# A graph-attention and mixture-of-experts layer: register loads without tests, accumulators read a step later, expert weights prepared earlier, another opening, and column groups of 8, 8, 8, 5 and 3 tiles

## The chip, the cores and the metric

One NeuronCore of one Trainium2 chip runs the whole kernel. The metric is device time in microseconds (us); less is better. Five engines work side by side, each on its own list in program order: TensorE (PE), VectorE (DVE), ScalarE (ACT), GpSimd (POOL) and SyncE (SP), which only issues transfers. They meet through semaphores alone.

## The reference

```python
def reference(x, adj, ...):            # x 4096 x 128, adj 4096 x 4096, int32, about 1% ones
    h  = layernorm(x)
    Wh = h @ W_w + W_b
    e  = leaky_relu((Wh @ a1)[:, None] + (Wh @ a2)[None, :], 0.2)
    x  = x + softmax(where(adj > 0, e, -9e15), axis=1) @ Wh
    h  = layernorm(x)
    top2, idx = top_k(h @ Wg.T + bg, 2)     # 8 experts, hidden width 512
    c  = softmax(top2) placed at idx
    return x + sum_e c[:, e] * (relu(h @ W1[e].T + b1[e]) @ W2[e].T + b2[e])
```

## The kernel before

**Attention.** The 4096 output rows are 32 column tiles of 128, taken in five supergroups of 8, 8, 8, 6 and 2 tiles (`WB`). Each supergroup goes through all 32 source tiles: 160 steps, numbered n. A step is one instruction on DVE, `weigh` (L779), which makes the unnormalised weights `prob` of one source tile against all columns of the supergroup, and on PE `attend` (L1283), one matmul per column tile into accumulators that stay in PSUM for the whole supergroup; fp32, so the profile has two passes for each. `prob` has 6 buffers, and DVE's list runs 4 steps ahead of PE's. The mask comes from the int32 adjacency: SP loads a chunk (2 steps of an 8- or 6-wide supergroup, 8 steps of the 2-wide one), and ACT turns it into bf16 (`edges`, L1111, its list 6 steps ahead). There are 4 chunk buffers and 4 mask buffers.

**The opening.** x is normalised, transposed (L1244, groups of four tiles), projected (L1251), and multiplied once more for the row term of the scores (L1255). ACT takes exponentials (`keep_s`), DVE stores `Wh` (`keep_Wh`). Groups 0 and 1 go through this ahead of step 0, groups 2 to 7 inside the steps of supergroup 0. A run-time flag, `narrow`, chooses between a short and a general way of making the weights; each engine loads it into a register and branches.

**End of a supergroup.** DVE adds the accumulators out of PSUM (`evacuate`, L849), and over the next 14 steps `finish` (parts p = 0 to 13, one a step) makes the rows x1, normalises them (xn, L885, at p = 4 and 5), has PE transpose them (L1397, p = 5 and 6), scores the experts (p = 7 and 8), ranks them, and writes slots, `offs` and `etab` (p = 11 to 13). PE cannot start the next supergroup before the accumulators are read, nor pass p = 5 before xn is there. Then POOL sends the rows to `xbuf` in DRAM, sorted by expert, with two indirect transfers for each column tile (`send`, L627, from 12 steps on; 8 steps on for the last supergroup, two to a step).

**Experts.** 71 tiles of 128 sorted rows (`NT`) follow, in five rounds; a round's tiles are those which are sure to be full after its supergroup, numbers 0, 9, 25, 41 and 53 being the first of each. SP loads a tile's rows (`load_slab`, L445 and L446) at a row number that it reads from `offs` into a register, five beats ahead of its use, six buffers; PE transposes (`turn`, L1323), multiplies up (L1351 to L1353) and down (L1370 to L1382); ACT and DVE split the hidden values into high and low fp16 parts (L1158, L996) and scale the result; POOL computes the target rows and scatters them to `ybuf` (`give_back`, L640). PE's work on a tile is cut into 14 pieces which lie between the matmuls of two steps. Tiles up to 35 are done that way. From step 160 on (`TAIL`, tile 36) a beat is one tile and nothing else, the last 35 tiles; and there SP also copies each tile's first-layer weights into the free mask buffers (`copy_weights`, L457 and L458), eight tiles ahead, at an address read from `etab`. PE reads the same table (`fetch`, L1331). The last supergroup's `finish` lies in steps 160 to 169.

**Other work put into the lists by step number.** Expert weights are loaded, shifted on POOL (L559), and split on ACT and DVE (L1121, L836) from step 20 + 6e on for expert e (`expert_at`). `add_bias` (L552, POOL) is at the steps of `bias_at`. In step 141 SP fills the ends of the expert regions with zeros (`fill_ends`, L431 and L432, eight transfers). At the end SP reads `ybuf` back, DVE adds, and the result is stored.

A register load with bounds is written `value_load(..., min_val=, max_val=)`.

Of the kernel before, what the change touches and what calls it, by code (L numbers as in the profile page):

```python
# [5 lines left out]
def build(nc, x, adjT, W, Wb, a, WgT, bg, wcat, wlast, b2, out):  # L6
# [7 lines left out]
    E = WgT.shape[1]  # L14
# [8 lines left out]
    WB = [8, 8, 8, 6, 2]  # L23
# [3 lines left out]
    STEPS = SG * TILES  # L27
    FW = F + 1
# [42 lines left out]
    chunks = [(g, u, min(8, 2 * SB // WB[g])) for g in range(SG) for u in range(0, TILES, min(8, 2 * SB // WB[g]))]  # L71
# [38 lines left out]
    with ctx:  # L110
# [194 lines left out]
        s_wlo = sem("s_wlo")  # L305
        s_G = sem("s_G")
# [87 lines left out]
        def _(sp):  # L394
# [11 lines left out]
            def load_chunk(m, general):  # L406
                if m >= AR:
                    if general:
                        sp.wait_ge(s_P, chunk_end[m - AR])
                    else:  # L410
                        sp.wait_ge(s_G, m - AR + 1)
# [23 lines left out]
            def load_slab(t):  # L435
# [9 lines left out]
                row = sp.value_load(offs[0:1, t:t + 1], min_val=0, max_val=ROWS - P)  # L445
                sp.dma_start(slab[t % XR][:, :], xbuf[bass.ds(row, P), :]).then_inc(s_ld[t % XR], 16)  # L446

            def copy_weights(t, general):
# [8 lines left out]
                e = sp.value_load(etab[0:1, t:t + 1], min_val=0, max_val=(E - 1) * EW)  # L457
# [42 lines left out]
            with sp.If(fast != 0):  # L500
                load_chunk(2, False)
                load_chunk(3, False)
                main(False)
            with sp.Else():
                for i in range(2):
                    sp.wait_ge(s_adj[i], 16)
                sp.wait_ge(s_G, 1)
# [181 lines left out]
        def _(dve):  # L689
# [34 lines left out]
            def keep_Wh(i):  # L724
# [19 lines left out]
            nc.vector.tensor_tensor(wsq[:, :], wa[:, 1:2], wa[:, 1:2], ALU.mult).then_inc(s_was, 1)  # L744
            nc.vector.tensor_copy(Wx[:, F:FW], wa[:, 1:2])
# [4 lines left out]
            normalise(1)  # L750
# [18 lines left out]
            def weigh(n):  # L769
# [6 lines left out]
                dve.wait_ge(s_G, m + 1)  # L776
# [5 lines left out]
            def row_maxima(g):  # L782

                if g == 0:
                    dve.wait_ge(s_whs, GROUPS)
                    dve.wait_ge(s_G, 1)
# [28 lines left out]
            def weigh_general(n):  # L815
# [13 lines left out]
                dve.wait_ge(s_adj[m % AR], 16 * (m // AR + 1 + (m % AR < 2)))  # L829
# [169 lines left out]
            def main(general):  # L999
                for n in range(-LB, NS):  # L1000
                    m = n + LB
                    ends = 0 <= n < STEPS and n % TILES == TILES - 1
                    if ends and not general:
                        evacuate(n // TILES)
                    if m < STEPS and (m or general):
                        (weigh_general if general else weigh)(m)
                    if ends and general:
                        evacuate(n // TILES)
                    if not general:
# [3 lines left out]
                        i = group_at(n, 3)  # L1013
# [478 lines left out]
```

## Time and profile before

| | us |
|---|---|
| median of 3 runs (lowest, highest) | 511.89 (507.74, 513.55) |
| the profiled execution, its own time | 510.71 |
| its span | 508.9 |
| PE busy, 4079 matmuls | 420.4 |
| DVE busy, 874 instructions | 361.3 |
| ACT busy | 259.6 |
| POOL busy | 238.3 |
| chain that ended last: PE 53%, SP's queue 13%, "issue" 12%, DVE 9%, DMA 6% | |

Supergroups 0 to 4 end on PE at about 101.2, 171.4, 261.5, 346.0 and 400.2 us. The last tile's result is ready at 484, and what follows is reading back, adding and storing. A busy share says little here, because each stretch has another limit: read the stretches one by one. SP has no busy time in the profile; its queue is seen only in the timeline and in the chain.

### The profile page before, as it was taken

The page shows a single profiled execution, that of the slowest core. Times are in us where ns is not written, and L with a number is a line of the kernel's source. Part 1 is how long each engine was busy: PE and PEld are TensorE (multiplying, and loading weights), DVE is VectorE, ACT ScalarE, POOL GpSimd, SP SyncE. Part 2 cuts the span into 40 slices and gives each one's busy share as a digit, 9 for nine tenths or more (in the row PEclk, how much of TensorE's full clock was granted, in tenths as well). Part 3 has the DMA queues.
Part 4 walks back from the last instruction along what each step waited for, and adds up shares of the span by engine and source line. Part 5 has one row for each costly group of instructions (what it writes and reads, how often), then busy time and mean ns, then how long its engine had stood idle before and what let it go on. Part 6 is the DMA issues. An engine that isn't in the chain of part 4 may idle for free.

```text
span 508.9 us, 12723 instructions
## 1 busy us (share of the span) xinstructions
PE 420.4 (83%) x4079; PEld 389.7 (77%) x4079; DVE 361.3 (71%) x874; ACT 259.6 (51%) x382; POOL 238.3 (47%) x298
## 2 busy tenths in 40 slices
PE   2679999977999759999997999998897986777800
PEld 1479999977999749999997999997886875555700
DVE  5297868999999998976659696547692668344526
ACT  2398678625746507554544745534643464455600
POOL 3412310513288420478824258873466648545510
PEclk9999999997999989999999999999898989999965
DMA  7889687983999835846462566513175545444258
GB/s 230 335 281 311 229 295 259 373 300 128 354 332 369 330 144 183 268 143 227 154 211 91 161 210 205 197 50 95 54 214 145 192 140 176 159 150 145 73 168 334
DMA packets 39164, 107.01 MB, mean 210 GB/s; under 512 B 6557, under 2 KB 17825, under 8 KB 32437
## 3 DMA queue, kind: packets, MB, share of 16 engines
q1 hardware_dynamic: 32468, 91.36, 53.0%
q0 software_dynamic: 4320, 8.47, 4.8%
q10 hardware_dynamic: 2304, 6.29, 3.6%
q8 instruction: 38, 0.62, 0.5%
q14 instruction: 34, 0.27, 0.2%
HBM read 84.57 MB, written 13.07 MB: 192 GB/s over the span
## 4 chain that ended last, share of the span: by engine, by line
PE 53%; SPq 13%; issue 12%; DVE 9%; DMA 6%; ACT 3%; POOL 3%; POOLq 0%; DVEq 0%; ACTq 0%
PE acc L1283 38%; DVE prob L779 3%; SPq L458 3%; DMA slab<-xbuf 2%; SPq L445 2%; SPq L457 2%; DMA adj<-ybuf 2%; PE yt L1251 2%; SPq L446 2%; PE m L1255 2%; POOL ybuf L640 2%; DMA adj<-adjT 1%; PE hps L1351 1%; PE hps L1353 1%; PE hps L1352 1%
## 5 line engine op out<-in xcount | busy, mean ns | idle before, releaser
L1283 PE MATMUL acc<-Wh,prob 128*128 128x129 f32 x2048 | 298.8, 288 | 4.7 <-DVE num L849 4.7
L1283 PEld LDWEIGHTS acc<-Wh,prob 128*128 128x128 f32 x2048 | 264.2, 195 | 9.6 <-issue 4.8
L779 DVE SCALAR_TENSOR_TENSOR prob<-s_bc,E_col,G_all 128x1024 f32<-128x1024 f32 (+2 forms) x160 | 178.8, 1136 | 24.0 <-PE acc L1283 22.8
L1111 ACT ACTIVATE G_all<-adj 128x2048 bf16<-128x2048 int32 (+1 forms) x68 | 122.1, 1803 | 22.7 <-DVE prob L779 16.2
L640 POOL DMA_INDIRECT ybuf<-wst,dest x71 | 74.1, 1043 | 72.7 <-ACT wst L1165 34.0
L627 POOL DMA_INDIRECT xbuf<-xr,slot x64 | 81.3, 1270 | 49.0 <-PE acc L1283 34.2
L996 DVE SCALAR_TENSOR_TENSOR wst<-hps,wst 128x512 f16<-128x512 f32 x71 | 49.0, 690 | 65.2 <-ACT wst L1158 63.8
L1158 ACT ACTIVATE wst<-hps 128x512 f16<-128x512 f32 x71 | 42.2, 594 | 18.5 <-PE hps L1353 14.7
L1153 ACT ACTIVATE xT<-yt 128x256 f16<-128x256 f16 x71 | 27.2, 382 | 32.4 <-PE yt L1323 31.8
L1165 ACT ACTIVATE wst<-yt,slab 128x128 f32<-128x128 f32 x36 | 13.2, 367 | 56.8 <-PE yt L1382 56.7
L559 POOL TENSOR_TENSOR wst<-wst,wlb 127x512 f32<-127x512 f32 x8 | 13.5, 1681 | 43.1 <-DMA wlb<-wlast 43.0
L1351 PE MATMUL hps<-xT,wall 128*128 128x128 f16 x148 | 32.6, 224 | 1.1 <-ACT xT L1153 0.6
L1353 PE MATMUL hps<-xT,wall 128*128 128x128 f16 x148 | 32.7, 224 | 0.0
L1352 PE MATMUL hps<-xT,wall 128*128 128x128 f16 x148 | 32.5, 223 | 0.0
L1323 PE MATMUL yt<-ident,slab 128*128 128x128 f16 x142 | 19.8, 221 | 15.0 <-DMA slab<-xbuf 14.0
L538 POOL TENSOR_TENSOR scratch<-scratch,mhalf 128x4 f32<-128x4 f32 x8 | 12.0, 1506 | 40.6 <-DVE scratch L713 40.6
L610 POOL TENSOR_TENSOR rstd<-ve,mhalf 128x4 f32<-128x4 f32 (+2 forms) x10 | 12.1, 1208 | 36.8 <-DVE ve L878 36.6
L1372 PE MATMUL yt<-wall,wst 128*128 x144 | 28.9, 225 | 0.0
L1370 PE MATMUL yt<-wall,wst 128*128 x144 | 28.7, 225 | 0.0
L1375 PE MATMUL acc<-wall,wst 128*128 x140 | 23.6, 283 | 4.7 <-issue 3.3
L1382 PE MATMUL yt<-wall,wst 128*128 x144 | 26.7, 220 | 0.0
L1323 PEld LDWEIGHTS yt<-ident,slab 128*128 128x128 f16 x142 | 11.8, 99 | 18.7 <-DMA slab<-xbuf 16.7
(177 smaller groups left out, 616.7 us busy)
## 6 DMA issues: line engine op xcount, KB each, us to landing
adj<-adjT SPq DMA_DIRECT2D x52, 1024.0 KB
adj<-adjT SPq DMA_DIRECT2D x16, 768.0 KB
G_all<-wall SPq DMA_DIRECT2D x34, 256.0 KB, 2.4
slab<-xbuf SPq DMA_DIRECT2D x71, 65.0 KB, 2.4
wst<-wcat ACTq DMA_DIRECT2D x8, 512.0 KB, 5.4
adj<-ybuf SPq DMA_DIRECT2D x8, 512.0 KB, 7.6
xs<-x SPq DMA_DIRECT2D x8, 256.0 KB, 9.4
wlb<-wlast ACTq DMA_DIRECT2D x8, 256.0 KB, 6.5
```

Of the source, the lines that this page charges most:

```text
L627: nc.gpsimd.indirect_dma_start(xbuf[:, :], bass.IndirectOffsetOnAxis(ap=slot[:, w, b:b + 1].bitcast(u32), axis=0), xr[:, w, b, :], None).t ...
L640: nc.gpsimd.indirect_dma_start(ybuf[:, :], bass.IndirectOffsetOnAxis(ap=dest[:, t:t + 1].bitcast(u32), axis=0), ysb[t % YR][:, :], None, b ...
L779: nc.vector.scalar_tensor_tensor(prob[n % PR][:, 0:w], c_bc[:, P * AT[g]:P * AT[g] + w], E_col[:, u:u + 1], G[m % GR][:, k * w:(k + 1) * w ...
L996: nc.vector.scalar_tensor_tensor(h_lo[t % 2][:, :], hps[t % 2][:, :], 0.0, h_hi[t % 2][:, :], op0=ALU.max, op1=ALU.subtract).then_inc(s_hl, 1)
L1111: nc.scalar.activation(G[m % GR][:, 0:w], adj_sb[m % AR][:, 0:w], ACT.Relu).then_inc(s_G, 1)
L1158: nc.scalar.activation(h_hi[t % 2][:, :], hps[t % 2][:, :], ACT.Relu).then_inc(s_hh, 1)
L1283: last = nc.tensor.matmul(acc_of(b), prob[n % PR][:, b * P:(b + 1) * P], Wh[:, u, :], start=(u == 0 and b % 3 == 0), stop=(u == TILES - 1) ...
L1323: last = nc.tensor.transpose(tps[:, h * P:(h + 1) * P], x16[:, h * P:(h + 1) * P], ident16[:, :])
L1351: nc.tensor.matmul(dst, whi, xhi, start=(k == 0), stop=False, skip_group_check=True)
L1352: nc.tensor.matmul(dst, whi, xlo, start=False, stop=False, skip_group_check=True)
L1353: last = nc.tensor.matmul(dst, wlo, xhi, start=False, stop=True, skip_group_check=True)
L1372: nc.tensor.matmul(yps, hi[:, ks], weights(t, 2 * HID + 2 * j * P + P), start=False, stop=False, skip_group_check=True)
```

## The change

Register loads of `offs` and `etab` carry their bounds as a statement and no longer as a test at run time (those of `fill_ends` stay). `evacuate` stands one step later in DVE's list, so the weights of one more step come ahead of it. Everything at `expert_at` comes 12 steps earlier, and `add_bias` 2 to 14 steps earlier. The last two supergroups are 5 and 3 tiles wide; the 3-wide one has chunks of 4 steps. The rounds then begin at tiles 0, 9, 25, 41 and 51. In the opening DVE makes the first mask, chunks 2 and 3 are asked for without a wait, the score row comes ahead of the projection, and the projection of group 1 and the work of groups 2 to 7 lie a step later in PE's list. The zero fill of `xbuf`'s spare rows moves from step 4 to step 64. (Column spans on the host follow; no arithmetic there.)

```diff
-    WB = [8, 8, 8, 6, 2]
+    WB = [8, 8, 8, 5, 3]
+    WIDE = [2, 2, 2, 2, 4]
-    chunks = [(g, u, min(8, 2 * SB // WB[g])) for g in range(SG) for u in range(0, TILES, min(8, 2 * SB // WB[g]))]
+    chunks = [(g, u, WIDE[g]) for g in range(SG) for u in range(0, TILES, WIDE[g])]
...
         def expert_at(n, part):
-            e, r = divmod(n - part - 20, 6)
+            e, r = divmod(n - part - 8, 6)
...
-        bias_at = {n: i for i, n in enumerate([28, 30, 58, 60, 90, 92, 122, 124])}
+        bias_at = {n: i for i, n in enumerate([26, 28, 44, 46, 84, 86, 116, 118])}
...  SP
-                row = sp.value_load(offs[0:1, t:t + 1], min_val=0, max_val=ROWS - P)
+                row = sp.value_load(offs[0:1, t:t + 1]).with_bounds(min_val=0, max_val=ROWS - P)
...
-                e = sp.value_load(etab[0:1, t:t + 1], min_val=0, max_val=(E - 1) * EW)
+                e = sp.value_load(etab[0:1, t:t + 1]).with_bounds(min_val=0, max_val=(E - 1) * EW)
...
-            for g in range(4, GROUPS):
+            load_chunk(2, False)
+            load_x(4)
+            load_chunk(3, False)
+            for g in range(5, GROUPS):
                 load_x(g)
...
-                    if n == 4:
+                    if n == 2 * TILES:
                         sp.wait_ge(s_const, 13)
                         sp.dma_start(xbuf[E * CAP:ROWS, :]...          # zero fill of spare rows
...  DVE
+            normalise(1)
             nc.vector.tensor_copy(Wx[:, F:FW], wa[:, 1:2])
...
-            normalise(1)
             dve.wait_ge(s_reach, 1)
...
+            dve.wait_ge(s_adj[0], 16)
+            nc.vector.tensor_scalar(G[0][:, :], adj_sb[0][:, :], 0.0, None, ALU.max).then_inc(s_G0, 1)
             stats(2)
-            stats(3)
...
-                    ends = 0 <= n < STEPS and n % TILES == TILES - 1
+                    ends = 0 < n <= STEPS and n % TILES == 0
                     if ends and not general:
-                        evacuate(n // TILES)
+                        evacuate(n // TILES - 1)
                     if m < STEPS and (m or general):
                         (weigh_general if general else weigh)(m)
...
-                        i = group_at(n, 3)
+                        i = 1 if n == -1 else group_at(n, 3)
                         if i is not None:
                             keep_Wh(i)
...
-                keep_Wh(0)
                 group_row(0)
                 weigh(0)
-                keep_Wh(1)
+                keep_Wh(0)
+                stats(3)
                 main(False)
...  ACT
-            def keep_s(i, general):
+            def keep_E(i):                 # the two exponentials of the projection
                 act.wait_ge(s_wh, i + 1)
...
+            def keep_s(i, general):        # the score row
                 act.wait_ge(s_sm, i + 1)
+                row = acc[2] if i == 1 else m1
...
-                        i = group_at(n, 1)
+                        i = group_at(n, 2)
                         if i is not None:
                             keep_hT(i)
-                        i = group_at(n, 2)
+                        if n == -1:
+                            keep_E(1)
+                        i = group_at(n, 3)
                         if i is not None:
+                            keep_E(i)
                             keep_s(i, general)
...
-            edges(0)
             keep_hT(0)
             keep_hT(1)
...  PE
+            transposes(0)
             pe.wait_ge(s_was, 2)
             nc.tensor.matmul(m1[:, P + 3:P + 4], ones[:, :], wsq[:, :], start=True, stop=True).then_inc(s_tq, 1)
-            transposes(0)
+            transposes(1)
             pe.wait_ge(s_was, 3)
             pe.wait_ge(s_tqs, 1)
+            project_s(0)
+            project_s(1)
             project(0)
-            transposes(1)
-            project(1)
...
-                place[t] = pe.value_load(etab[0:1, t:t + 1], min_val=0, max_val=(E - 1) * EW)
+                place[t] = pe.value_load(etab[0:1, t:t + 1]).with_bounds(min_val=0, max_val=(E - 1) * EW)
...
-                        i = group_at(n, 0)
+                        i = group_at(n, 1)
                         if i is not None:
                             transposes(i)
-                        i = group_at(n, 2)
+                        if n == 1:
+                            project(1)
+                        i = group_at(n, 3)
                         if i is not None:
                             project(i)
+                            project_s(i)
```

## Rows read from the trace of the kernel before

**Rows 1.** Stages: length, busy us per engine (instructions), granted PE clock, DMA share, GB/s.
```profile
29.23:101.20 71.97, 71.97 (x595) 68.92 (x594) 59.10 (x89) 56.15 (x73) 18.40 (x20) 1.00 0.86 295
101.20:171.40 70.20, 62.56 (x546) 62.01 (x545) 68.07 (x141) 37.20 (x25) 35.14 (x26) 0.95 0.84 308
261.50:346.00 84.50, 80.85 (x856) 77.80 (x854) 59.44 (x153) 42.22 (x66) 49.38 (x54) 1.00 0.50 157
346.00:400.20 54.20, 46.27 (x486) 41.63 (x484) 36.10 (x132) 24.14 (x45) 30.99 (x39) 0.94 0.46 135
400.20:485.80 85.60, 65.87 (x799) 51.90 (x796) 45.61 (x130) 45.23 (x107) 48.87 (x77) 0.98 0.43 143
```
**Rows 2.** Chain of waits, start and length in us: one register test on SP.
```profile
426.11 0.15 SPq L445
...
426.38 0.04 SPq L446
```
**Rows 3.** Instructions of line 499, the load of the flag, written without bounds.
```profile
L499 SPq TENSOR_LOAD <-narrow x1: 471/471/471, 12.4 to 12.4; - x1
```
**Rows 4.** Two stretches of the last 35 tiles, columns as in rows 1.
```profile
440.00:470.00 30.00, 22.13 (x268) 16.67 (x267) 12.08 (x24) 15.37 (x36) 14.49 (x24) 1.00 0.46 151
474.00:480.00 6.00, 5.93 (x82) 4.92 (x81) 3.43 (x7) 4.09 (x11) 2.77 (x5) 1.00 0.27 68
```
**Rows 5.** SP's timeline (start, length): row loads of tiles 40, 41, 51 and 67.
```profile
395.83 0.35 SPq L446 DMA_DIRECT2D slab<-xbuf  x1
...
404.14 0.33 SPq L446 DMA_DIRECT2D slab<-xbuf  x1
...
430.29 0.35 SPq L446 DMA_DIRECT2D slab<-xbuf  x1
...
472.21 0.35 SPq L446 DMA_DIRECT2D slab<-xbuf  x1
```
**Rows 6.** POOL's timeline: three of the last four sends; then their median time to landing.
```profile
422.17 0.96 POOL L627 DMA_INDIRECT xbuf<-xr,slot  x1 [0.30 <-issue]
...
426.18 0.96 POOL L627 DMA_INDIRECT xbuf<-xr,slot  x1 [0.30 <-issue]
427.44 0.95 POOL L627 DMA_INDIRECT xbuf<-xr,slot  x1 [0.30 <-issue]
...
xbuf<-xr,slot POOLq DMA_INDIRECT x4, 2.6
```
**Rows 7.** Chain of waits: an unbroken run of PE passes in supergroup 0.
```profile
83.12 12.51 PE acc L1283 x112
```
**Rows 8.** PE's timeline where it stood still (in brackets how long, and for whom).
```profile
174.66 9.17 PE L1283 MATMUL acc<-Wh,prob 128*128 128x129 f32 x80 [3.25 <-DVE num L849]
190.07 1.12 PE L1397 MATMUL m<-ident,xn 128*128 128x128 f32 x4 [6.24 <-DVE xn L885]
...
386.54 0.29 PE L1323 MATMUL yt<-ident,slab 128*128 128x128 f16 x2 [2.96 <-DMA slab<-xbuf]
```
**Rows 9.** Timeline of the opening: mask 0, x group 2, steps 0 and 1, projection 2.
```profile
11.07 1.91 ACT L1111 ACTIVATE G_all<-adj 128x2048 bf16<-128x2048 int32 x1 [6.40 <-DMA adj<-adjT]
...
26.64 1.64 ACT L1078 ACTIVATE xn<-xs,nm,scratch 128x128 f32<-128x128 f32 x4
...
29.23 5.46 PE L1283 MATMUL acc<-Wh,prob 128*128 128x129 f32 x32
34.53 1.06 PE L1251 MATMUL yt<-Wx,xnT 128*128 128x129 f32 x8
```
**Rows 10.** POOL adds a bias; DVE's two weighings then; the first of them alone.
```profile
163.44 1.48 POOL L552 TENSOR_TENSOR xs<-xs,Wb_row 128x512 f32<-128x512 f32 x1
162.52 3.49 DVE L779 SCALAR_TENSOR_TENSOR prob<-s_bc,E_col,G_all 128x1024 f32<-128x1024 f32 x2
162.52 1.27 DVE L779 SCALAR_TENSOR_TENSOR prob<-s_bc,E_col,G_all 128x1024 f32<-128x1024 f32 x1
```
**Rows 11.** The stretch with the highest DMA share in supergroup 0, columns as in rows 1.
```profile
36.00:40.00 4.00, 4.00 (x36) 3.76 (x35) 3.38 (x5) 3.70 (x7) 1.60 (x3) 1.00 1.07 266
```
**Rows 12.** A group of DVE instructions: an expert's low parts (busy us, mean ns).
```profile
L836 DVE SCALAR_TENSOR_TENSOR wall<-wst,wall 128x1024 f16<-128x1024 f32 x8 | 11.9, 1485 | 0.0
```

More of the change, by code:

```diff
@@ L305, in build @@
         s_wlo = sem("s_wlo")
+        s_G0 = sem("s_G0")
         s_G = sem("s_G")
@@ L409, in load_chunk @@
                         sp.wait_ge(s_P, chunk_end[m - AR])
+                    elif m == AR:
+                        sp.wait_ge(s_G0, 1)
                     else:
-                        sp.wait_ge(s_G, m - AR + 1)
+                        sp.wait_ge(s_G, m - AR)
                 if general:
@@ L500, in _ @@
             with sp.If(fast != 0):
-                load_chunk(2, False)
-                load_chunk(3, False)
                 main(False)
             with sp.Else():
-                for i in range(2):
+                for i in range(AR):
                     sp.wait_ge(s_adj[i], 16)
-                sp.wait_ge(s_G, 1)
+                sp.wait_ge(s_G0, 1)
                 main(True)
@@ L775, in weigh @@
                 m, w = chunk_of[n], P * WB[g]
-                dve.wait_ge(s_G, m + 1)
+                if m:
+                    dve.wait_ge(s_G, m)
+                elif n == 0:
+                    dve.wait_ge(s_G0, 1)
                 ge(dve, s_at, n - PR + 1)
@@ L1007, in main @@
                     if ends and general:
-                        evacuate(n // TILES)
+                        evacuate(n // TILES - 1)
                     if not general:
@@ L1062, in _ @@
                 for i in range(2, GROUPS):
-                    if i >= 4:
+                    if i >= 3:
                         stats(i)
@@ L1097, in keep_s @@
                                      bias=bE[:, :], scale=1.0 - SLOPE).then_inc(s_ED, 1)
+            def keep_s(i, general):
                 act.wait_ge(s_sm, i + 1)
+                row = acc[2] if i == 1 else m1
                 if general:
-                    nc.scalar.activation(s_bc[:, i * GW:(i + 1) * GW], m1[:, :], ACT.Identity,
+                    nc.scalar.activation(s_bc[:, i * GW:(i + 1) * GW], row[:, :], ACT.Identity,
                                          bias=wa[:, 2:3]).then_inc(s_sbc, 1)
                 else:
-                    nc.scalar.activation(c_bc[:, i * GW:(i + 1) * GW], m1[:, :], ACT.Exp, bias=bC[:, :],
+                    nc.scalar.activation(c_bc[:, i * GW:(i + 1) * GW], row[:, :], ACT.Exp, bias=bC[:, :],
                                          scale=-(1.0 - SLOPE)).then_inc(s_sbc, 1)
@@ L1223, in _ @@
             with act.If(fast != 0):
-                for i in range(2):
-                    keep_s(i, False)
+                keep_s(0, False)
+                keep_s(1, False)
+                keep_E(0)
                 main(False)
             with act.Else():
+                keep_s(0, True)
+                keep_s(1, True)
                 for i in range(GROUPS):
@@ L1230, in _ @@
                         keep_hT(i)
-                    keep_s(i, True)
+                    keep_E(i)
+                    if i >= 2:
+                        keep_s(i, True)
                 main(True)
@@ L1253, in project, with project_s @@
                 last.then_inc(s_wh, 1)
-                ge(pe, s_sbc, i)
-                nc.tensor.matmul(m1[:, :], wa1_bc[:, :], hT[i % 2][:, :], start=True, stop=True).then_inc(s_sm, 1)
+            def project_s(i):
+                pe.wait_ge(s_hT, i + 1)
+                if i >= 2:
+                    pe.wait_ge(s_sbc, i)
+                row = acc[2] if i == 1 else m1
+                nc.tensor.matmul(row[:, :], wa1_bc[:, :], hT[i % 2][:, :], start=True, stop=True).then_inc(s_sm, 1)
             pe.wait_ge(s_WTs, 1)
@@ L1278, in attend @@
                     pe.wait_ge(s_whs, u // GT + 1)
+                if n == 0:
+                    pe.wait_ge(s_sbc, 2)
                 for b in range(WB[g]):
@@ L1446, in _ @@
             with pe.Else():
+                project(1)
                 for i in range(2, GROUPS):
@@ L1449, in _ @@
                     project(i)
+                    project_s(i)
                 main(True)
@@ L1468 @@
     N = np.asarray(x).shape[0]
-    spans = [(0, 8), (8, 16), (16, 24), (24, 30), (30, 32)]
+    spans = [(0, 8), (8, 16), (16, 24), (24, 29), (29, 32)]
     rows1 = np.concatenate([W1.transpose(2, 0, 1)[:F - 1], b1[None]], axis=0)
```

6 lines of the change are left out of this document (2 added, 4 removed).

## The prediction, made before the changed kernel ran

> **What bounds the kernel now.** I read the page's chain of waits first. Its shares (PE 53%, SP's queue 13%, issue 12%) say that no single engine sets the time, so I cut the span at the ends of the supergroups and read each piece [rows 1]. The reader is to see four different limits. In supergroup 0 PE is busy for the whole 71.97 us: every microsecond by which it starts earlier arrives at its end. In supergroup 1 PE has 62.56 of 70.20 us and DVE 68.07: DVE is nearly full, and PE stands at its edges. In supergroup 3 PE has 80.85 of 84.50. In the narrow supergroup 4 it has only 46.27 of 54.20, at a mean granted clock of 0.94, so there is time in which PE waits or runs at 1.2 instead of 2.4 GHz.
>
> The last 35 tiles are the odd stretch: PE has 65.87 of 85.60 us. A tile there is 23 matmuls. In the thirty microseconds from 440 there were 268 of them, 11.65 tiles, 2.57 us a tile; from 474, when SP has nothing left to issue, 82 in 6 us, 3.57 tiles, 1.68 us a tile [rows 4]. PE could do a tile in 1.68 and gets one in 2.57. Row loads of tiles 41 and 67 were issued at 404.14 and 472.21, 26 tiles in 68.07 us, 2.62 each [rows 5], and the chain of waits runs along SP's queue from one to the other. So SP's list is the limit: for each tile a row load and a weight copy, each with a register load, a test and the issue of the transfer.
>
> **The tests.** On the chain the test begins at 426.11 and the next thing that the transfer needs, its address, at 426.38 [rows 2]: 0.27 us for one. The duration shown is 0.15; the remainder is what lies between SP's instructions, and it goes too. That a load without bounds has no such work is seen at line 499, which has one instruction only [rows 3]. Two a tile make 0.54, and the pace becomes 2.62 - 0.54 = 2.07 us, still above PE's 1.68. From tile 41 to 67 that could be 26 x 0.54 = 14.1 us. I do not take it whole, because of the next part. On PE the tests are costed at nothing: inside the steps its register loads run ahead of the array, hidden under the matmuls (cover gone, 0.27 a tile, 38 tiles). The eight tests in `fill_ends` stay.
>
> **What the width 5 and 3 does to the last round.** The last round now begins at tile 51 instead of 53, and has six sends instead of four. They lie on POOL in steps 168, 169 and 170, two each, between give-backs. Before, the first pair began at 422.17 and the second at 426.18, the last send at 427.44, landing 2.6 us after its issue [rows 6], and SP's pace shows no gap for it. Now a third pair comes one round of POOL later, 426.18 - 422.17 = 4.0 us; the supergroup's `finish` has three tiles instead of two (I take 0.5 more); the attention behind tile 34 has nine steps with two more passes each, and a pass costs 12.51 / 112 = 0.112 us [rows 7], so 2.0 us. With 0.5 for SP's register load, tile 51 is asked for at 427.44 + 4.0 + 0.5 + 2.0 + 2.6 + 0.5 = 437.0 in the old frame (both frames laid together at the load of tile 40, 395.83), against 430.29 [rows 5]. That is a new wait of 6.7 us ahead of tile 51; behind it on SP's list stand all later loads and copies, and PE waits for them. Whatever SP saved before tile 51 is lost in it. From 51 to 67 it saves 16 x 0.54 = 8.7. Net for the last 35 tiles: **-2.0**. Bounds: -11 when the sends don't gate at all, +7 when only the wait comes and no saving.
>
> **Supergroup 3** loses one of six column tiles: 32 steps x 2 passes x 0.112 = 7.15 us of PE's work, where PE is nearly always the limit [rows 1]. A little turns into waiting in the first ten steps, where `finish` sets the pace: **-6.0** (-3 to -8; the upper end has the smaller number of switches between fp32 and fp16 passes).
>
> **Supergroup 4** gets the same 7.15 back, in a place with cover. Of it 5.1 us (23 steps) come ahead of tile 34. Idle PE time is 7.93 us, and a clock of 0.94 over the stage is worth some 3 more [rows 1]. The largest stand is for tile 35's rows, 2.96 us [rows 8], because SP is held by `fill_ends`; seven longer steps now run beside those eight transfers and take 1.6 us from it, and a short stand also leaves the clock up. `finish` has five tiles instead of six. I let 7.1 of the 11 be filled: 5.1 - 7.1 = **-2.0** (-5 to +3).
>
> **Accumulators a step later.** PE's stand at step 37 waits for xn, and DVE works without a pause from reading the accumulators to xn. The weighing that now lies ahead of the reading falls into DVE's own waiting time at the end of supergroup 0: 1.27 us [rows 10], **-1.3** (-2.3 to 0). Where DVE is late itself, as at 174.66 [rows 8], it moves PE's wait from one stand to the other and gives nothing. In supergroups 3 and 4 it is inside the terms above.
>
> **Expert weights from step 8.** The last two experts' low parts leave the stretch from step 56 to 69, 2 x 1.49 us [rows 12], and with them come two collisions less with POOL, each 1.0 us: while POOL added a bias, the first of two weighings took 1.27 us and both together 3.49 [rows 10], so the second one took 1.0 longer. PE's stands there are 3.25 and 6.24 us [rows 8], all for DVE. I take 4.0 off them. The new place of the low parts is supergroup 0, where DVE has 59.10 of 71.97 us [rows 1] and room for two more. But biases 2 and 3 go to steps 44 and 46, just ahead of the steps where DVE's lead over PE is smallest; I put 1.0 against it. Net **-3.0** (-5.5 to +1).
>
> The Trainium skill ("SBUF — State Buffer", section "SBUF: two separate sides") has the port pair that VectorE and GpSimd share as an exclusive lock for the whole instruction. By that rule a weighing caught by a bias would lose up to its 1.48 us instead of the 1.0 of the row, two of them 3 us, and this part would give 2 instead of 3.
>
> **The opening.** Laying out the new lists with the old durations: the first mask (1.91 us, and 6.40 of waiting before it) is off ACT [rows 9], transposes and score rows follow one another, the two group-0 exponentials end near 18.5 us, step 0 begins near 21 instead of 29.23. Then ACT is the limit: mask, x group 2 (1.64), mask, a wait for projection 1 near 26, two exponentials, mask, x group 3, mask, copy, which is 32.9 us. There projection 2 starts with three steps behind it; before, it started at 34.53 with two [rows 9]. Gain 1.6 and one step of 16 passes, 1.8: **-3.4** (-1 to -5.5; the clock of the first steps is open by a step's doubling, 1.8). From there on PE bounds again. The zero fill's move, chunks 2 and 3, and the shorter, more numerous chunks of supergroup 4 are hidden by four buffers; if that cover goes, it is the fourth rival.
>
> **Sum.** -2.0 - 6.0 - 2.0 - 1.3 - 3.0 - 3.4 = -17.7 on the profiled execution's 510.71, 493.0. The median of the runs lies 1.2 above it, so **494**.
>
> **Rivals.** *The sends don't gate.* POOL could fall in step sooner, and landing takes what it takes; then the 6.7 us wait goes, and SP's queue pays back up to 9 us: 485. For it: POOL has free time in that stage, 48.87 busy of 85.60 [rows 1]. Against: the give-backs between the pairs, which wait for finished tiles [rows 6]. Chance 0.13.
>
> *The tests don't go away*, because what line 445 shows as fused register work is partly the address. Then the wait ahead of tile 51 stands alone: -17.7 + 8.7 = -9.0, 503. Against: line 446 has its own such instruction [rows 2], and line 499 has none. 0.08.
>
> *DVE becomes the bound of supergroup 1*, full as it is at 68.07 of 70.20 [rows 1]: the earlier biases cost 2 more and the 3.0 is not earned, 494 + 5 = 499. 0.09.
>
> *Transfers become the bound of supergroups 0 and 1.* Two experts' weights more, 1.5 MB, go through supergroup 0, with 295 GB/s x 71.97 us = 21.2 MB already there. At the lowest rate seen with full DMA engines, 266 GB/s [rows 11], the 22.8 MB take 85.6 us, +13.6, and supergroup 1's 308 x 70.2 less 1.5 MB take 75.5, +5.3: -17.7 + 18.9 = +1.2, **513**, slower than before. It decides when masks come later than the three chunks in hand. For it: a DMA share of 0.86 [rows 1]. Against: that 266 was at the zero fill's short rows, which leave. 0.06, half of it beyond 1%.
>
> **Chances and range.** Forecast 0.62, its own range 488 to 500; the rivals as given; 0.02 for none of them. 484 to 504 holds forecast, both nearest rivals and most of the first. One per cent, 5 us, is about what a measurement tells from no change here: faster by more 0.90, within 0.05 (half of the transfers' case, the edge of the tests'), slower 0.05.
>
> **What would show it.** No test instruction at the two SP lines, and 0.27 less between load and address. Row loads of tiles 52 to 67 every 2.07 us, and a gap of SP ahead of tile 51 ended by the sends' landing, with PE idle for 6 to 9 us beside it. Step 0 near 21 us but projection 2 only near 33. PE's stands around 174 and 190 shorter by 4 together. Supergroup 3 near 78 us. No stand of more than 2 us for tile 35. The forecast is wrong if tile 51 comes without a gap, if the pace stays at 2.6, or if masks are late in supergroup 0.

## The result, and the profile after

The changed kernel took 488.62 us (median of 4 runs, 486.83 to 492.72), the kernel before in the same series 510.47: ratio 0.958, 95% interval 0.949 to 0.967. The forecast was 494, its range 484 to 504. The profiled execution of the changed kernel took 492.72 with a span of 491.0, so 18.0 less than the 510.71 profiled before, where the sum had 17.7. That execution is the slowest of the changed kernel's four, though: the medians lie 21.9 apart, with an interval that has room for 17.7. Of all executions below, one (of the kernel with late expert weights, 507.45) was in the chip's slower state, and the medians leave it out.

That the sum is right says nothing yet of its terms. The span cut at the same places in both profiles (ends of steps on PE, row loads of tiles 40 and 67 on SP):

| stretch | before | after | difference | forecast |
|---|---|---|---|---|
| start to the end of supergroup 0 | 101.2 | 99.2 | -2.0 | -3.4 |
| supergroups 1 and 2 | 160.3 | 156.0 | -4.3 | -1.3 - 3.0 |
| supergroup 3 | 84.5 | 77.3 | -7.2 | -6.0 |
| from there to the load of tile 40 | 49.8 | 45.4 | -4.4 | -2.0 |
| load of tile 40 to load of tile 51 | 34.5 | 41.8 | +7.3 | +6.7 |
| load of tile 51 to load of tile 67 | 41.9 | 33.3 | -8.6 | -8.7 |
| from there to the end | 36.7 | 38.0 | +1.3 | 0 |

The stages of the changed kernel (length, busy us of PE, PE's weight loads, DVE, ACT and POOL with instructions in brackets, granted PE clock, DMA share, GB/s), and one piece of the last of them:

```profile
18.02:99.20 81.18, 74.75 (x606) 70.93 (x606) 64.39 (x104) 60.48 (x81) 28.25 (x45) 0.96 0.88 317
99.20:169.70 70.50, 63.22 (x546) 62.44 (x545) 67.67 (x141) 38.69 (x26) 33.53 (x26) 0.95 0.85 289
255.20:332.50 77.30, 73.28 (x786) 70.49 (x784) 57.04 (x153) 40.32 (x67) 45.04 (x54) 0.98 0.51 150
332.50:384.70 52.20, 47.55 (x550) 45.26 (x548) 37.79 (x124) 26.63 (x48) 30.86 (x41) 1.00 0.61 193
384.70:466.70 82.00, 64.60 (x803) 57.11 (x800) 45.44 (x137) 44.73 (x107) 50.12 (x75) 0.90 0.42 138
410.00:420.00 10.00, 4.85 (x51) 4.35 (x50) 5.80 (x17) 3.01 (x8) 8.00 (x12) 0.83 0.46 162
```

Against [rows 1]: supergroup 1 is not shorter (70.50 against 70.20), since its gain falls just behind its end, in steps 64 and 69. The narrow supergroup has the full clock now. The last stage is 3.6 shorter, and yet it contains a stretch in which PE has 4.85 us of 10 and a granted clock of 0.83.

The tests are gone. Chain of waits, one of SP's row loads (L450) with the register load (L449) ahead of it:

```profile
438.21 0.28 SPq L449
438.49 0.04 issue
438.52 0.04 SPq L450
```

Nothing but 0.04 us lies between the register and the address, where [rows 2] have the test. SP's timeline for tiles 40, 51 and 67, as in [rows 5]; the last line holds tiles 67 and 68:

```profile
377.94 0.34 SPq L450 DMA_DIRECT2D slab<-xbuf  x1
...
419.72 0.34 SPq L450 DMA_DIRECT2D slab<-xbuf  x1
...
453.02 1.29 SPq L450 DMA_DIRECT2D slab<-xbuf  x2
```

From tile 51 to 67 a tile takes 33.3 / 16 = 2.08 us. Ahead of tile 51 there is the new gap. What SP waited for between its loads of tiles 40 and 51 (us in total, times, longest), and POOL's last sends:

```profile
SPq L447 <- DVE wst L999: 8.3, 6, 2.1
SPq L448 <- DMA xbuf<-xr,slot: 4.5, 1, 4.5
...
SPq L461 <- DVE offs L984: 1.0, 1, 1.0
```
```profile
411.66 0.96 POOL L632 DMA_INDIRECT xbuf<-xr,slot  x1 [0.31 <-issue]
...
415.67 0.96 POOL L632 DMA_INDIRECT xbuf<-xr,slot  x1 [0.30 <-issue]
416.93 0.96 POOL L632 DMA_INDIRECT xbuf<-xr,slot  x1 [0.30 <-issue]
```

The pairs follow each other by 4.01 us, as the two pairs of [rows 6] did, and tile 51 is asked for 2.8 us after the last send's issue. In the kernel before SP shows no wait at all in the same stretch. Now it has four kinds: for a row buffer to come free, for the sends, for a weight buffer (1.6 us), and for the tables that `finish` writes. The sends are the last of them and hold tile 51, but for 4.5 us only; without them it could have been asked for near 415.3. PE's side of it:

```profile
412.91 0.61 PE L1407 MATMUL acc<-wall,wst 128*128 x4 [2.87 <-DVE wst L1005]
...
421.57 0.28 PE L1348 MATMUL yt<-ident,slab 128*128 128x128 f16 x2 [3.85 <-DMA slab<-xbuf]
```

Two stands, 6.7 us together. Those answering to [rows 8], in PE's timeline:

```profile
170.44 9.17 PE L1308 MATMUL acc<-Wh,prob 128*128 128x129 f32 x80 [0.74 <-DVE num L858]
...
183.53 0.90 PE L1422 MATMUL m<-ident,xn 128*128 128x128 f32 x4 [3.92 <-DVE xn L894]
...
369.76 0.29 PE L1348 MATMUL yt<-ident,slab 128*128 128x128 f16 x2 [1.15 <-DMA slab<-xbuf]
```

9.49 us have become 4.66 behind supergroup 1, and 2.96 have become 1.15 for tile 35. In the opening, against [rows 9]:

```profile
18.02 2.02 PE L1308 MATMUL acc<-Wh,prob 128*128 128x129 f32 x16 [2.94 <-DVE Wh L734]
...
31.37 2.09 PE L1268 MATMUL yt<-Wx,xnT 128*128 128x129 f32 x8 [6.42 <-ACT xnT L1094]
33.25 1.92 PE L1277 MATMUL m<-xnT,scratch 128*128 128x512 f32 x2
```

Step 0 starts 11 us earlier, and PE then stands 6.42 us for ACT, whose masks wait 3.8 us in sum (2.02, 0.82 and 0.96) for their chunks. Projection 2 comes at 31.37, and takes 2.09 us at the lower clock level where [rows 9] have 1.06.

### The profile page after: what moved, and what is told of

Read it like the earlier page. It is cut to its first block, busy times and chain, and to the rows that moved or that the text cites. A ratio compares the mean times of both kernels' runs of the same rounds, so it can differ in the third digit from the quotient of the medians.

```text
span 491.0 us, 12388 instructions
## 1 busy us (share of the span) xinstructions
PE 411.5 (84%) x4079; PEld 390.6 (80%) x4079; DVE 359.3 (73%) x875; ACT 256.8 (52%) x385; POOL 236.4 (48%) x298
## 3 DMA queue, kind: packets, MB, share of 16 engines
q0 software_dynamic: 4320, 8.47, 5.0%
## 4 chain that ended last, share of the span: by engine, by line
PE 57%; issue 10%; SPq 9%; DVE 9%; DMA 7%; POOL 4%; ACT 2%; POOLq 0%; ACTq 0%; DVEq 0%
PE acc L1308 40%; DMA adj<-adjT 3%; DVE prob L788 3%; DMA adj<-ybuf 2%; PE hps L1376 2%; PE hps L1378 2%; PE hps L1377 2%; SPq L462 2%; PE yt L1268 1%; POOL ybuf L645 1%; PE m L1429 1%; SPq L450 1%; PE m L1277 1%; PE acc L1400 1%; POOL rstd L615 1%
## 5 line engine op out<-in xcount | busy, mean ns | idle before, releaser
L788 DVE SCALAR_TENSOR_TENSOR prob<-s_bc,E_col,G_all 128x1024 f32<-128x1024 f32 (+2 forms) x160 | 175.3, 1116 | 15.4 <-PE acc L1308 14.9
L1121 ACT ACTIVATE G_all<-adj 128x2048 bf16<-128x2048 int32 (+2 forms) x71 | 121.0, 1712 | 22.1 <-DVE prob L788 16.8
L632 POOL DMA_INDIRECT xbuf<-xr,slot x64 | 76.6, 1197 | 47.1 <-PE acc L1308 32.7
L564 POOL TENSOR_TENSOR wst<-wst,wlb 127x512 f32<-127x512 f32 x8 | 14.2, 1774 | 36.9 <-DMA wlb<-wlast 36.9
L1376 PE MATMUL hps<-xT,wall 128*128 128x128 f16 x148 | 30.9, 221 | 0.3 <-issue 0.3
L1378 PE MATMUL hps<-xT,wall 128*128 128x128 f16 x148 | 31.0, 222 | 0.0
L1377 PE MATMUL hps<-xT,wall 128*128 128x128 f16 x148 | 30.9, 222 | 0.0
L543 POOL TENSOR_TENSOR scratch<-scratch,mhalf 128x4 f32<-128x4 f32 x8 | 13.2, 1647 | 35.0 <-DVE scratch L718 35.0
L1397 PE MATMUL yt<-wall,wst 128*128 x144 | 27.5, 220 | 0.0
L1395 PE MATMUL yt<-wall,wst 128*128 x144 | 27.4, 220 | 0.0
L1378 PE MATMUL hps<-xT,G_all 128*128 128x128 f16 x136 | 27.2, 233 | 0.0
L1377 PE MATMUL hps<-xT,G_all 128*128 128x128 f16 x136 | 27.2, 233 | 0.0
L1376 PE MATMUL hps<-xT,G_all 128*128 128x128 f16 x136 | 27.2, 233 | 0.0
L615 POOL TENSOR_TENSOR rstd<-ve,mhalf 128x4 f32<-128x4 f32 (+3 forms) x10 | 12.2, 1219 | 30.9 <-DVE ve L887 30.7
```

The source lines that it names most:

```text
L632: nc.gpsimd.indirect_dma_start(xbuf[:, :], bass.IndirectOffsetOnAxis(ap=slot[:, w, b:b + 1].bitcast(u32), axis=0), xr[:, w, b, :], None).t ...
L788: nc.vector.scalar_tensor_tensor(prob[n % PR][:, 0:w], c_bc[:, P * AT[g]:P * AT[g] + w], E_col[:, u:u + 1], G[m % GR][:, k * w:(k + 1) * w ...
L1121: nc.scalar.activation(G[m % GR][:, 0:w], adj_sb[m % AR][:, 0:w], ACT.Relu).then_inc(s_G, 1)
L1376: nc.tensor.matmul(dst, whi, xhi, start=(k == 0), stop=False, skip_group_check=True)
L1377: nc.tensor.matmul(dst, whi, xlo, start=False, stop=False, skip_group_check=True)
L1378: last = nc.tensor.matmul(dst, wlo, xhi, start=False, stop=True, skip_group_check=True)
```

## The experiments

Twelve runs follow: parts of the change done alone or undone, one by one or together, two of them run again, and the changed kernel once more. The first four share one chip with each other (the kernel before: 510.37 us), the other eight share another, on which the kernel before took 520.2. Medians are compared within a chip only; the changed kernel's own 488.62 stands beside the first four by the kernel before of its series, 510.47.

| kernel | us | ratio to before, 95% interval |
|---|---|---|
| first chip: before | 510.37 | |
| before, tests taken out | 497.65 | 0.9755 (0.9702 to 0.9807) |
| changed, SP's tests back | 499.81 | 0.9793 (0.9741 to 0.9845) |
| changed, widths 6 and 2 | 489.39 | 0.9589 (0.9521 to 0.9657) |
| changed, last sends together | 487.62 | 0.9553 (0.9499 to 0.9607) |
| second chip: before | 520.2 | |
| changed | 501.16 | 0.9651 (0.9607 to 0.9695) |
| changed, expert weights late | 502.29; 504.31 | 0.9606 (0.9528 to 0.9684); 0.9706 (0.9672 to 0.9741) |
| changed, accumulators read early | 507.59; 507.77 | 0.9715 (0.9643 to 0.9787); 0.9773 (0.9731 to 0.9814) |
| changed, x late | 501.26 | 0.9607 (0.9549 to 0.9666) |
| x late, sends together | 501.75 | 0.9665 (0.9636 to 0.9694) |
| x late, sends together, 6 and 2 | 501.80 | 0.9627 (0.9564 to 0.9690) |

### The tests alone

```diff
-sp.value_load(offs[0:1, t:t + 1], min_val=0, max_val=ROWS - P)
+sp.value_load(offs[0:1, t:t + 1]).with_bounds(min_val=0, max_val=ROWS - P)
```
In the kernel before, here and at the two loads from `etab`, on SP and on PE.

> The kernel before, with nothing changed but the run-time tests of the register loads of `offs` and `etab`. Theory (SP's queue is the limit of the last 35 tiles, 0.54 us a tile): row loads every 2.07 us instead of 2.62; a small wait ahead of tile 53, the first of the old last round, because its four sends land near 430; some 12 us less than before, no change ahead of 395 us. Rival 1 (no gate at all): 14 to 16 us less. Rival 2 (SP's queue only looks like the limit, PE or the transfers are): under 3 us less, and the pace stays near 2.6.

497.65, which is 12.7 less. Supergroup 3 ends at 346.2, as before at 346.0. SP's row loads of tiles 40 and 67:

```profile
393.69 0.34 SPq L446 DMA_DIRECT2D slab<-xbuf  x1
...
458.82 0.34 SPq L446 DMA_DIRECT2D slab<-xbuf  x1
```

Tile 41 is asked for at 399.88, 4.3 us earlier than in [rows 5], tile 67 13.4 us earlier. So the tests are run-time work, as the forecast had it, and they also cost 2.1 us ahead of tile 40, which it had not counted: from tile 35 on SP is already the late one. The small wait that was expected ahead of tile 53 isn't there: the last send is issued at 422.98 and tile 53 asked for at 428.17.

### The tests back in the changed kernel

The diff above reversed, on SP's two lines.

> The changed kernel with the tests put back on SP's two lines (PE's stay away). Theory (what SP saves ahead of tile 51 is lost in the wait for the last sends, what it saves from 51 to 67 counts): 16 x 0.54 = 8.7 us more than the changed kernel, 13 less than before, all of it after tile 51's load; row loads 2.6 us apart. Rival (the whole saving counts): 14 us more, 8 less than before.

499.81, 11.2 above the changed kernel's 488.62. Tile 51 and tile 67 on SP's timeline:

```profile
418.06 0.35 SPq L450 DMA_DIRECT2D slab<-xbuf  x1
...
461.14 0.35 SPq L450 DMA_DIRECT2D slab<-xbuf  x1
```

43.1 us for 16 tiles against 33.3, which is 9.8 where 8.7 was expected. (The two profiled spans are 7.0 us apart and not 11.2, as the changed kernel's is that of its slowest execution.) And tile 51 is not later than in the changed kernel (418.06 against 419.72; supergroup 0 ended 0.9 earlier here), though SP came to tile 40 with the tests' 2.1 us lost. So what SP does faster ahead of that tile turns into waiting; this was the central claim about the last round, and here it is shown. Most of it isn't the wait for the sends, however. With the tests, SP waited for these between tiles 40 and 51:

```profile
SPq L448 <- DMA xbuf<-xr,slot: 3.5, 1, 3.5
...
SPq L447 <- DVE wst L999: 0.7, 1, 0.7
```

Without them it waits 1.0 us more for the sends and 7.6 more for row buffers, which come free when DVE has scaled a tile's result (L999).

### The widths back

```diff
-    WB = [8, 8, 8, 5, 3]
+    WB = [8, 8, 8, 6, 2]
```
with the chunk sizes and column ranges that belong to it.

> The changed kernel with supergroups of 8, 8, 8, 6 and 2 tiles and chunks of eight steps in the last. Theory (5 and 3 gains in supergroups 3 and 4 and pays with the wait ahead of the last round): supergroup 3 longer by 7, supergroup 4 shorter by 3 to 4, the wait ahead of the last round shorter by 6 to 8; the whole within 3 us of the changed kernel. Rival (the widths are what makes the change fast): 6 to 10 us more than the changed kernel.

489.39 against 488.62. Tiles 40, 51 and 67 on SP's timeline:

```profile
386.23 0.34 SPq L450 DMA_DIRECT2D slab<-xbuf  x1
...
417.72 0.34 SPq L450 DMA_DIRECT2D slab<-xbuf  x1
...
451.70 0.46 SPq L450 DMA_DIRECT2D slab<-xbuf  x1
```

At tile 40 this kernel is 8.3 us behind the changed one, at tile 51 it is 2.0 ahead: it needs 31.5 us between them, the changed kernel 41.8. Supergroup 0 ended 1.2 us earlier in this profile. Allowing for that, the changed kernel leads by 9.5 at tile 40, and nothing of it is left at tile 51, where it is 0.8 behind, nor at tile 67, where it is 0.1 behind. The narrow supergroup, which was expected to be 3 to 4 us shorter with two tiles, takes 52.6 us against 52.2: with two tiles PE has 64 passes less, and again a mean granted clock of 0.94 instead of 1.00. Here tile 53 is the first that needs the last sends, and SP shows no wait for them.

### The last six sends together

```diff
-    PACE = [(1, 1)] * 4 + [(1, 2)]
+    PACE = [(1, 1)] * 4 + [(1, 6)]
```

> The changed kernel with all six sends of the last supergroup in step 168, one after another, ahead of the give-backs of that step, instead of two each in steps 168 to 170. Theory (tile 51 waits for the landing of the last send, which waits behind two give-backs): last send 2.5 to 3 us earlier, tile 51's load and everything after it 2.5 to 3 us earlier. Rival (tile 51 waits for something else: the tile table, or PE): no change, and the load of tile 51 where it was.

487.62 against 488.62, intervals overlapping. POOL's first and last send, then SP's load of tile 51:

```profile
406.33 0.96 POOL L632 DMA_INDIRECT xbuf<-xr,slot  x1 [0.30 <-issue]
...
412.63 0.96 POOL L632 DMA_INDIRECT xbuf<-xr,slot  x1 [0.31 <-issue]
```
```profile
416.05 0.34 SPq L450 DMA_DIRECT2D slab<-xbuf  x1
```

Last send 4.3 earlier, tile 51 3.7 earlier, span 4.0 shorter in that one execution: in the profile the sends gate (SP waits 2.2 us for them, behind its four weight copies). The medians do not confirm a gain of 4.

### Expert weights late again

```diff
-        e, r = divmod(n - part - 8, 6)
+        e, r = divmod(n - part - 20, 6)
```
with `bias_at` as before.

> The changed kernel with the expert weights from step 20 and the biases at their old steps. Theory (PE's two stands at the end of supergroup 1 are DVE's lateness): the stands at steps 64 and 69 longer by 2.5 and 2.2 us, a step near 50 without its stand of 1.2; 3 to 4 us more in all, everything ahead of step 45 alike. Rival (DVE would be late anyway): under 1 us more.

502.29, from three executions that lie 7 us apart. The changed kernel on the same chip:

> The changed kernel once more, so that three variants beside it can be read against it on one chip. Theory: ratio to the kernel before 0.958 as at first (between 0.949 and 0.967), with the wait ahead of tile 51 and row loads from tile 51 to 67 in 33 us. Rival: the first ratio was helped by its chip, 0.965 to 0.975.

501.16, ratio 0.9651: at the edge of both expectations, and 0.958 itself lies a little below its interval. On this chip the last part runs slower (step 127 ends at 330.4, but step 159 at 389.1 instead of 384.7), and from tile 51 to 67 it took 34.9 us instead of 33.3. SP does not always issue there as it did on the first chip; the combinations below show it. The pair side by side:

> Once more the changed kernel with the expert weights' steps and the biases where the kernel before has them, now with the changed kernel beside it on the same chip. Theory: 3 to 4 us slower than the changed kernel (step 64 near 7.7 us long against 2.8, step 50 without its stand). Rival: the stretch is only shifted between steps 50, 64 and 101, and the total is within 1.5 us.

504.31, 3.1 more than the changed kernel, with intervals that overlap; the earlier run was only 1.1 above it. PE behind supergroup 1, in this kernel and in the changed one on the same chip:

```profile
167.07 11.40 PE L1308 MATMUL acc<-Wh,prob 128*128 128x129 f32 x80 [4.23 <-DVE num L858]
...
181.28 0.66 PE L1422 MATMUL m<-ident,xn 128*128 128x128 f32 x4 [2.82 <-DVE xn L894]
```
```profile
166.69 9.17 PE L1308 MATMUL acc<-Wh,prob 128*128 128x129 f32 x80 [0.74 <-DVE num L858]
...
179.76 1.11 PE L1422 MATMUL m<-ident,xn 128*128 128x128 f32 x4 [3.91 <-DVE xn L894]
```

The stand in front of `num` also lowers the clock: 80 passes take 11.40 us instead of 9.17. Steps 64, 69 and 70 take 17.1 us against 14.2 here and 13.0 in the first profile of the changed kernel. Against it stand 1.15 us in step 50 (2.94 against 1.79), 0.4 in steps 52 to 55, and 1.3 at the first stand for xn, in steps 37 and 38. With 0.6 gained elsewhere, 0.7 is left from step 3 to step 70. The earlier profile of this kernel has 18.8 us for steps 64, 69 and 70 and 0.5 instead of the 1.3, and 3.6 are left. Supergroup 0 from step 4 to its end takes 61.2 us with late weights and 61.3 with early ones.

### Accumulators read early again

```diff
-ends = 0 < n <= STEPS and n % TILES == 0
+ends = 0 <= n < STEPS and n % TILES == TILES - 1
```
and `evacuate(n // TILES)`.

> The changed kernel with the reading of the accumulators at its old place, ahead of the weighing of the step three further on. Theory (that weighing fell into DVE's own waiting): PE's waits for xn longer by 1.27 us in supergroup 1 and 2, by 0.85 and 0.6 in 3 and 4, partly filled; 2 to 4 us more. Rival (it only moves the wait from one stand to the other): no change beyond 0.5 us.

> Once more the changed kernel with the accumulators read in the last step of their supergroup, not in the first of the next, beside the changed kernel on the same chip. Theory: 3 to 4 us slower, 0.7 to 1.7 at each of the four edges. Rival: only the edge behind supergroup 0 counts, 1 us slower or less, as the prediction's term of 1.3 had it.

507.59, and beside the changed kernel 507.77, which is 6.6 more: the forecast's 1.3 is far too low, and the 3 to 4 of the theory probably too. PE's stands for xn behind supergroups 0, 1 and 2, in this kernel, and in the changed one on the same chip:

```profile
114.39 1.11 PE L1422 MATMUL m<-ident,xn 128*128 128x128 f32 x4 [6.71 <-DVE xn L894]
...
184.34 1.12 PE L1422 MATMUL m<-ident,xn 128*128 128x128 f32 x4 [5.11 <-DVE xn L894]
...
270.55 0.65 PE L1422 MATMUL m<-ident,xn 128*128 128x128 f32 x4 [3.24 <-DVE xn L894]
```
```profile
110.99 1.12 PE L1422 MATMUL m<-ident,xn 128*128 128x128 f32 x4 [5.52 <-DVE xn L894]
...
265.69 0.66 PE L1422 MATMUL m<-ident,xn 128*128 128x128 f32 x4 [2.44 <-DVE xn L894]
```

1.19, 1.20 (5.11 against the 3.91 of the row at 179.76 above) and 0.80 less: one weighing's length each time, also where DVE was the late one (at 184). With 0.50 at step 133 that is 3.7 us that the profile shows in place. Behind the third of these stands there is more: steps 101 and 102 take 10.15 us against 7.72, in both profiles of this kernel. The stretch from step 101 to 102 in this kernel and in the changed one, columns as in the stages above:

```profile
267.30:277.40 10.10, 6.86 (x58) 6.51 (x57) 5.98 (x21) 4.03 (x7) 5.62 (x7) 0.83 0.36 117
```
```profile
263.20:270.90 7.70, 5.26 (x58) 5.09 (x57) 5.25 (x17) 4.02 (x7) 5.31 (x7) 1.00 0.35 106
```

After 3.24 us of standing PE's clock fell, after 2.44 it did not, and that is the 1.6 beyond the 0.80. But it isn't this edit's for certain: in its first profile the changed kernel (9.37 us), and beside it the one with late weights (9.36), lost the clock there after 2.45 and 2.44 us as well. The rest of the 6.6 I can't place. Some 2 us come back in supergroup 4, and this profile has 5 us more in steps 125 and 126, with PE's instructions 0.7 us apart and nothing waited for; the earlier one of the same kernel has not, the one of the next experiment has 4.

### x asked for later

```diff
-            load_x(4)
             load_chunk(3, False)
-            for g in range(5, GROUPS):
-                load_x(g)
```
and groups 4 and 5 behind chunk 4, 6 and 7 behind chunk 5.

> The changed kernel with x groups 4 to 7 (1 MB) asked for behind adjacency chunks 4 and 5 instead of ahead of chunk 4. In the changed kernel step 3 waited: chunk 4's mask came at 28.83 because the chunk was 14.45 us on its way. Theory (the opening is now bound by what the transfers bring by then): chunk 4 lands 2.5 to 3 us earlier, projection 2 and all steps from 3 on start 2.5 to 3 us earlier. Rival (ACT's own list is the limit): under 1 us.

Step 3 ended at 35.1 instead of 37.9, yet the changed kernel itself ends it at 34.2 on this chip, and the medians are 501.26 and 501.16. The order of these loads makes no difference that can be measured.

### Combinations

The edits above together, with widths 5 and 3, and with 6 and 2.

> The changed kernel with two edits together: x groups 4 to 7 asked for behind chunks 4 and 5, and all sends of the last round of slab writes in one place of POOL's list. Theory: both edits act on paths that set the end, the opening's 1 to 3 us (step 3 ends near 36 us instead of 37.9) and the 4 us by which the last send came earlier, so 4 to 6 us faster than the changed kernel beside it, ratio near 0.948. Rival: what the opening gives is eaten by DVE, which sets the end of supergroup 1, and the profiled 4 us of the sends were a chance alignment of POOL: within 1.5 us of the changed kernel.

> The changed kernel with x late, the last sends together, and widths 6 and 2. Theory: x late brings 2.5 to 3, the sends nearly nothing here (four sends, tile 53), the widths within 3: between 482 and 488 us. Rival (the gains don't add, the transfers taken from the opening come back as late masks): 488 to 492.

501.75 and 501.80 against 501.16: nothing gained, neither the 4 to 6 us nor the 482 to 488. In the first of the two the last send is issued at 417.28, 3.4 us earlier than in the changed kernel on this chip (420.7), and still tile 51 is asked for at 423.3 against 423.5. SP's four weight copies ahead of tile 51, and that tile's load:

```profile
414.20 8.47 SPq L462 DMA_DIRECT2D G_all<-wall  x4
423.26 0.34 SPq L450 DMA_DIRECT2D slab<-xbuf  x1
```

It isn't the sends that hold tile 51 here: SP shows no wait for them, and the load follows 0.6 us behind the last copy. The four copies themselves take 8.47 us. In the changed kernel's first profile they took

```profile
410.98 3.63 SPq L462 DMA_DIRECT2D G_all<-wall  x4
```

The chain of waits has SP's instructions 0.7 us long or 0.7 us apart between these copies, with nothing waited for:

```profile
418.26 0.71 SPq L461
418.97 0.81 issue
```

Such stretches are in all eight profiles from the second chip (in the changed kernel's too, between 413 and 423) and in none of the other six. So the combination can't show here what the landing of the sends costs, and on the first chip it wasn't run. No version beat the changed kernel beyond what a measurement can tell.

## Why the prediction was right

**The tests (-8.7, and 0.27 us each): right.** Pace 2.08 us, and with the tests back 43.1 us for the 16 tiles. On the second chip the same 16 tiles take 33.9 to 36.4 us without the tests. The rival in which they are partly address work falls, since taking them out alone gives 12.7 us.

**The wait ahead of tile 51 (+6.7): right, +7.3.** It was the one term that turned a large saving into a small one, and it came out of two rows: the distance of two pairs of sends, and their landing. Counted from the load of tile 40 as in the forecast, tile 51 comes at 437.6, where it had 437.0. The rival in which the sends don't gate falls by SP's waits of 4.5, 3.5 and 2.2 us for them in the three profiles from outside the second chip that have six sends at the end. Its price was too high all the same: 9 us, where the 4.5 are all that the changed kernel could have got, since row buffers and tables held SP just before. The forecast had neither of these two waits.

**Supergroup 3 (-6.0): -7.2.** With the old widths it takes 83.4 us (255.0 to 338.4) in the changed kernel, with the new ones 77.3: 6.1 for the widths. Most of the rest is the accumulators' 0.8 at its sixth step. **Supergroup 4 (-2.0): -4.4**, because the tests' 2.1 us ahead of tile 40 weren't counted; they are seen alone in the first experiment and again in the second (47.5 us instead of 45.4 from the end of supergroup 3 to that tile). The remaining 2.3 are the term as it was. The extra did not reach the end in full, as tile 51 waits for the sends. So the new widths as a whole, worked out as -6.0 - 2.0 + 6.7 = -1.3, measure -0.8 in the medians, which is within the noise, and nothing in the profiles.

**Expert weights (-3.0): borne out, but not closely.** The medians give 3.1 and 1.1, neither clear of the noise; up to step 70 the profiles show 0.7 and 3.6 net. The 4.0 off the stands was 3.0 and 4.6, the 1.0 for the earlier biases was 1.15, in step 50. The room in supergroup 0 for two more low parts was there, as they cost 0.1. What lies between 0.7 and 3.6 is mostly at the edges, in stands and in the clock behind them, and two profiles can't say which is the rule. How a caught weighing is priced can be read in the changed kernel's timeline of POOL (an expert's shift) and of DVE:

```profile
144.82 1.49 POOL L564 TENSOR_TENSOR wst<-wst,wlb 127x512 f32<-127x512 f32 x1
```
```profile
145.09 2.30 DVE L788 SCALAR_TENSOR_TENSOR prob<-s_bc,E_col,G_all 128x1024 f32<-128x1024 f32 x1
```

Alone it takes 1.28, so it lost 1.0. POOL had 1.22 us left when it began, and POOL's own instruction was not lengthened. The Trainium skill ("SBUF — State Buffer", section "SBUF: two separate sides") has an exclusive lock for the whole instruction: this agrees with the row within 0.2 us, if the loss is what the other instruction still had to run; the up to 1.48 that I had weighed would need the weighing to begin with it.

**Accumulators (-1.3, and more inside the terms of supergroups 3 and 4): mis-sized, 6.6 in the medians.** The step that failed is "where DVE is late itself, as at 174.66, it moves PE's wait from one stand to the other and gives nothing". At 184 it gives 1.20 as at 114, since what has left the chain from the reading to xn is a whole weighing, wherever DVE stands. The profile bears out 3.7 of the 6.6, of which 2.4 belong to the term's own two edges.

**The opening (-3.4): -2.0.** Step 0 was placed 3 us too late (18.0 against 21) and projection 2 1.5 too late (31.4 against 32.9), with the three steps behind it as foreseen. What was left out of the sum, though not out of its range, is the clock. PE stood 6.42 us; columns as in the stages above, the stretch behind that stand, and then the same piece of work in the execution on the second chip, where PE had stood 3.22 us:

```profile
31.40:33.20 1.80, 1.80 (x8) 1.80 (x9) 0.00 (x0) 0.00 (x0) 0.00 (x0) 0.50 0.95 355
```
```profile
30.50:31.50 1.00, 1.00 (x9) 1.00 (x10) 0.67 (x1) 0.00 (x0) 0.84 (x3) 1.00 1.07 377
```

A granted clock of 0.50, the lower of the two levels (1.2 GHz), against 1.00: projection and row term took 2.09 and 1.92 us against 1.16 and 1.02, and the two steps behind them 4.73 against 3.73. That is 2.8 us from the clock and 3.2 from the stand itself, and step 3 took 12.95 us in the one and 7.03 in the other. There projection 2 stands at

```profile
30.44 1.16 PE L1268 MATMUL yt<-Wx,xnT 128*128 128x129 f32 x8 [3.22 <-ACT xnT L1094]
```

and supergroup 0 ended at 95.6 instead of 99.2. The opening varies by more than its term was worth.

**The end (0): +1.3.** From tile 67's load to the last give-back nothing changed (13.6 and 13.7 us). From there to the end it is 23.1 before and 24.3 after. On the first chip it is 23.8 to 24.2 in the three variants of the changed kernel and 23.2 in the kernel before without tests, on the second 22.2 to 23.5. Part of it may be the change's; no run isolates it.

One row was read too simply. From 474 to 480, where the forecast took PE's own pace of 1.68 us a tile, SP still issued row loads until 476.3; only the weight copies had ended. No term hangs on it.

So the closeness of the total is luck, by errors that cancel: 3.6 more than forecast in supergroups 3 and 4, against 1.4 less in the opening, 0.6 more of waiting, 0.1 of pace and 1.3 at the end.

## What to carry to other kernels

Where an engine only issues transfers, count its instructions between two of them and multiply: a bounds test of 0.27 us was worth 12 us here, on a queue that has no busy time in the profile. Before a saving on such a queue is added up, look for the next things in it that wait for another engine (a transfer's landing, a buffer that must come free), since what is saved ahead of such a point goes into the wait. And between an engine's last input and its result that another one stands for, each foreign instruction counted in full, at all four edges and not only where its engine seemed idle.

## What had not been expected of the hardware

- **Landing of indirect transfers.** Where SP issues at its usual pace, from issue of the last send to the load that waits for it: 2.8 and 3.1 us with the sends in pairs, 3.4 when six were issued 1.27 us apart. Issuing them 4.3 us sooner brought the load 3.7 sooner.
- **A queue that slows down by itself.** On the second chip SP's instructions come 0.7 us apart in places, with nothing waited for: four weight copies took 8.47 us instead of 3.63. No run shows why.
- **The clock behind a stand.** After 6.42 us of standing PE ran at 0.50, after 3.22 in the same place at 1.00. But behind supergroup 2 stands of 2.44 to 2.45 us were followed by the lower level in two profiles and not in two others. And the last stage ran at a mean granted clock of 0.90 (0.98 before), with 0.83 in the ten microseconds around the two stands: part of what the wait costs isn't idle time but slower matmuls.
- **Two chips.** The kernel before takes 510.4 us on one and 520.2 on the other, the changed one 488.6 and 501.2. Gains of a few us can only be compared within a chip.
